# A new order of the lead and of the side steps of a four-row hybrid block

## The reference

```python
x = x + attn_a(layernorm(x))   # per token: q, k, v by heads, elu, k*v summed over heads, q*(kv), two RMS norms, an MLP
x = x + ffn(layernorm(x))      # router, softmax, top 8 of 32 experts, sum of w_e * down(silu(gate) * up)
x = x + attn_b(layernorm(x))   # causal attention, 16 heads of 8, window of 64
x = x + ffn(layernorm(x))
```

## Time and profile before

| what | us |
|---|---|
| median of 3 runs | 997.12 (996.98 to 1001.0) |
| the profiled execution | 996.92 |
| its span, first to last instruction | 995.20 |

### The profile page before, as it was taken

How to read it: one execution, slowest core, us unless ns; L and a number is a source line. 1 busy time by engine, 2 the same in 40 slices (tenths; PEclk the granted TensorE clock), 3 DMA queues, 4 the chain that set the end, 5 groups by cost and what they waited for, 6 DMA issues and landing times.

```text
span 995.2 us, 16822 instructions
## 1 busy us (share of the span) xinstructions
PE 898.2 (90%) x5456; PEld 619.3 (62%) x5456; DVE 663.5 (67%) x1471; ACT 610.0 (61%) x1875; POOL 672.2 (68%) x617
## 2 busy tenths in 40 slices
PE   3276889899999999999999999999999998999998
PEld 1043556677666666587666666677666666767665
DVE  5988777688858747788638846778735347547532
ACT  4344566895665665796674566798465478386432
POOL 7566959576778848766759857856755646645654
PEclk8557999999999999999999999999999999999999
DMA  5004333113442433610433534430334561350352
GB/s 188 0 1 109 73 88 87 43 45 92 104 126 54 123 101 94 158 45 27 95 87 87 129 85 99 128 84 18 73 100 88 127 156 28 78 138 12 85 130 64
DMA packets 64903, 85.75 MB, mean 86 GB/s; under 512 B 5232, under 2 KB 30768, under 8 KB 64560
## 3 DMA queue, kind: packets, MB, share of 16 engines
q1 hardware_dynamic: 64816, 84.68, 35.1%
HBM read 79.39 MB, written 5.28 MB: 85 GB/s over the span
## 4 chain that ended last, share of the span: by engine, by line
PE 55%; ACT 12%; POOL 9%; DVE 6%; issue 5%; DMA 0%; DVEq 0%; SPq 0%; ACTq 0%; POOLq 0%
PE bank L1563 15%; PE bank L1540 8%; PE bank L1542 8%; PE bank L1541 8%; ACT probs L1102 6%; PE bank L1584 3%; POOL work L893 3%; PE bank L1599 3%; PE bank L1613 2%; POOL rstd L837 1%; PE bank L1577 1%; PE bank L1427 1%; DVE work L1325 1%; DVE probsT L1367 1%; POOL kv_terms L850 1%
## 5 line engine op out<-in xcount | busy, mean ns | idle before, releaser
L893 POOL TENSOR_TENSOR work<-work,spread_w 128x512 f32<-128x512 f32 x256 | 336.2, 1324 | 163.8 <-DVE work L1325 160.7
L1325 DVE TENSOR_TENSOR work<-work,bank 128x512 f32<-128x512 f32 x256 | 173.7, 682 | 214.3 <-ACT work L1077 129.3
L1563 PE MATMUL bank<-work,down_w 128*128 128x512 f32 x512 | 263.9, 599 | 12.0 <-POOL work L893 10.0
L1077 ACT ACTIVATE work<-bank 128x512 f32<-128x512 f32 x256 | 150.8, 596 | 177.0 <-PE bank L1542 173.5
L1540 PE MATMUL bank<-z_hi,gate_hi 128*128 128x512 f32 x256 | 166.5, 650 | 5.6 <-ACT work L1077 3.6
L1102 ACT ACTIVATE probs<-bank,neg_max 128x96 f32<-128x96 f32 x512 | 166.0, 383 | 5.8 <-DVE neg_max L1353 3.9
L901 POOL TENSOR_TENSOR probs<-probs,prob_inv 128x768 f32<-128x768 f32 x64 | 94.1, 1471 | 67.5 <-DVE prob_inv L1361 67.5
L1102 ACT ACTIVATION_READ_ACCUMULATOR probs<-bank,neg_max 128x1 f32 x512 | 126.4, 250 | 0.0
L1563 PEld LDWEIGHTS bank<-work,down_w 128*128 128x128 f32 x512 | 94.1, 189 | 44.4 <-POOL work L893 18.1
L1542 PE MATMUL bank<-z_hi,gate_lo 128*128 128x512 f32 x256 | 102.2, 399 | 0.0
L1540 PE MATMUL bank<-z_hi,up_hi 128*128 128x512 f32 x256 | 102.0, 399 | 0.0
(11 more groups left out here) (155 smaller groups left out, 1477.3 us busy)
## 6 DMA issues: line engine op xcount, KB each, us to landing
spread_w<-comb_dram SPq DMA_DIRECT2D x96, 512.0 KB, 6.6
spread_w<-comb_dram SPq DMA_DIRECT2D x128, 128.0 KB, 3.0
vals<-v_dram SPq DMA_DIRECT2D x16, 384.0 KB, 4.1
...
```

The lines of the kernel that those rows point to most:

```text
L893: pool.tensor_tensor(work[:, n % WORK], work[:, n % WORK], spread_w[:, n // EACH % 2, s % EACH], ALU.mult).then_inc(hid_gated, 1)
L1077: act.activation(work[:, n % WORK], bank[GATE_BANKS[ring_of(row, f, s)]], ACT.Silu).then_inc(silu_ready, 1)
L1325: dve.tensor_tensor(work[:, n % WORK], work[:, n % WORK], bank[UP_BANKS[ring_of(row, f, s)]], ALU.mult).then_inc(gated_ready, 1)
L1563: pe.matmul(bank[Y_BANK], down_w[:, c], work[:, n % WORK], start=(c == 0), stop=(c == CH - 1)).then_inc(down_done, 1)
```

## The change

Only the two tables `PLAN` and `AHEAD` are written anew. Both hold the same 655 steps, and no function changes. `AHEAD` has 123 steps instead of 120: `qscale` 0, `attend` 1 and `kvsum` 0 of the next row come in from the first stage. The parts that the prediction speaks of:

```diff
     (0, "first"): {
-        0: own(("h_pow2", 1)) + ahead(("kvsum", 0)) + own(("h_newton2", 1)),
-        1: own(("h_scale", 1)) + ahead(("qscale", 0)) + own(("h_gain", 1)),
-        2: ahead(("wterm", 0)),
-        3: own(("h_sum", 1), ("x_add", 1)) + ahead(("attend", 1), ("wred", 0), ("kvsum", 1)),
-        6: own(("attnT", 1), ("mlp1", 1)),
-        7: own(("mlp2", 1), ("m_stats", 1), ("m_rstd", 1)) + ahead(("wterm", 1)),
-        8: ahead(("wred", 1), ("attend", 2)) + own(("m_apply", 1)) + ahead(("x_stats", 1), ("x_rstd", 1)),
-        10: own(("moe_turn", 1), ("z_hi", 1), ("z_lo", 1)) + ahead(("attend", 3), ("kvsum", 2), ("wterm", 2)),
-        11: ahead(("wred", 2)) + own(("route", 1), ("r_sum", 1), ("top", 1)),
-        12: ahead(("x_apply", 1)) + own(("weigh", 1)) + ahead(("kvsum", 3), ("x_turn", 1)) + own(("comb", 1)),
-        13: ahead(("qkv", 4), ("wterm", 3)),
-        14: own(("cnorm", 1), ("weighT", 1)),
-        15: ahead(("qkv", 5), ("wred", 3)),
+        2: own(("h_pow2", 1), ("h_newton2", 1), ("h_scale", 1)),
+        4: own(("h_gain", 1), ("h_sum", 1)) + ahead(("wterm", 0), ("wred", 0), ("kvsum", 1)) + own(("x_add", 1)),
+        6: own(("attnT", 1), ("mlp1", 1)),
+        7: own(("mlp2", 1), ("m_stats", 1), ("m_rstd", 1)),
+        8: ahead(("wterm", 1)),
+        9: ahead(("x_stats", 1), ("x_rstd", 1)) + own(("m_apply", 1)),
+        10: own(("moe_turn", 1)) + ahead(("attend", 2), ("attend", 3)) + own(("z_hi", 1), ("z_lo", 1)),
+        11: ahead(("wred", 1)) + own(("route", 1), ("r_sum", 1), ("top", 1)) + ahead(("x_apply", 1)) +
+            own(("weigh", 1)) + ahead(("kvsum", 2)),
+        12: ahead(("x_turn", 1)) + own(("comb", 1)),
+        13: ahead(("qkv", 4), ("wterm", 2)) + own(("cnorm", 1)),
+        14: ahead(("wred", 2)) + own(("weighT", 1)) + ahead(("kvsum", 3), ("wterm", 3)),
+        15: ahead(("qkv", 5)),
     },
     (0, "third"): {
-        0: ahead(("h_sq1", 0), ("h_g2", 0), ("h_red1", 0), ("h_newton1", 0), ("h_sq2", 0), ("qkv", 6),
-            ("h_red2", 0), ("h_pow2", 0)),
-        1: ahead(("h_newton2", 0), ("qkv", 7)),
-        3: ahead(("expo", 1)) + own(("y_back", 0), ("s_stats", 0)) + ahead(("h_scale", 0)) + own(("s_rstd", 0)) +
-            ahead(("elu", 1)),
...
+        0: ahead(("wred", 3), ("h_sq1", 0), ("h_red1", 0), ("h_g2", 0), ("h_newton1", 0), ("qkv", 6), ("h_sq2", 0)),
+        1: ahead(("h_red2", 0), ("qkv", 7), ("h_pow2", 0), ("h_newton2", 0)),
+        3: own(("y_back", 0), ("s_stats", 0)) + ahead(("h_scale", 0), ("h_gain", 0), ("h_sum", 0)) +
+            own(("s_rstd", 0)),
+        4: ahead(("expo", 1), ("elu", 1)),
...
     },
     (0, "attn"): {
-        0: ahead(("moe_turn", 0), ("z_hi", 0)),
-        2: ahead(("z_lo", 0)),
...
-        20: own(("proj", 0)) + ahead(("cnorm", 0)),
-        22: ahead(("weighT", 0)),
+        0: ahead(("wred", 4), ("wterm", 5), ("z_hi", 0)),
+        1: ahead(("z_lo", 0)),
+        2: own(("y_back", 1), ("s_stats", 1), ("s_rstd", 1)),
+        4: ahead(("wred", 5)) + own(("s_apply", 1)),
...
+        22: own(("proj", 0)),
+        23: own(("m_stats", 2), ("m_rstd", 2)),
+        25: ahead(("weighT", 0)),
     },
     (1, "third"): {
...
-        6: ahead(("x_turn", 1), ("h_red2", 0), ("h_pow2", 0)),
-        7: back(("moe_turn", 3), ("z_hi", 3)) + ahead(("h_newton2", 0)),
-        8: back(("z_lo", 3)) + ahead(("h_scale", 0)),
-        9: back(("route", 3), ("r_sum", 3)) + ahead(("h_gain", 0)),
...
+        6: back(("moe_turn", 3), ("z_hi", 3), ("z_lo", 3)),
...
+        9: back(("route", 3), ("r_sum", 3)) + ahead(("h_gain", 0)) + back(("top", 3), ("weigh", 3)),
...
     },
     (1, "fourth"): {
...
-        7: ahead(("z_lo", 0), ("wterm", 5), ("attend", 6)),
-        8: ahead(("route", 0), ("r_sum", 0)) + own(("s_apply", 1)),
-        9: own(("seq_turn", 1)) + ahead(("top", 0), ("wred", 5)) + own(("bias", 1)),
...
-        12: ahead(("cnorm", 0), ("wred", 6)),
-        13: ahead(("weighT", 0), ("kvsum", 7)),
...
+        7: ahead(("route", 0), ("attend", 6), ("attend", 7), ("r_sum", 0), ("top", 0), ("kvsum", 5), ("wterm", 5),
+            ("wred", 5)),
...
+        10: ahead(("comb", 0), ("wterm", 6), ("wred", 6)) + own(("keys", 1)) + ahead(("cnorm", 0)),
...
     },
     (1, "attn"): {
-        8: back(("y_back", 3)),
-        26: own(("proj", 0)),
+        0: ahead(("weighT", 0)),
+        5: back(("y_back", 3)),
+        9: ahead(("wred", 7)) + own(("bias", 1)) + ahead(("h_sq1", 1)),
+        13: ahead(("h_g2", 1)),
+        15: ahead(("h_red1", 1), ("h_sq2", 1)),
+        26: ahead(("h_newton1", 1)),
     },
     (2, "attn"): {
-        8: back(("y_back", 3)),
-        26: own(("proj", 0)),
+        0: ahead(("weighT", 0), ("kvsum", 7)) + own(("bias", 1)),
+        2: ahead(("wterm", 7)) + back(("y_back", 3)),
+        6: ahead(("wred", 7)),
+        10: ahead(("h_sq1", 1)),
+        11: ahead(("h_g2", 1)),
+        14: ahead(("h_red1", 1)),
+        23: ahead(("h_newton1", 1)),
     },
     (3, "first"): {
-        0: back(("m_stats", 2), ("m_rstd", 2)) + own(("h_sq1", 1), ("h_g2", 1)),
-        1: own(("h_red1", 1)),
-        2: own(("h_newton1", 1), ("h_sq2", 1)),
-        3: back(("proj", 1)) + own(("h_red2", 1), ("h_pow2", 1)),
...
+        1: back(("proj", 0)),
+        2: own(("h_sq2", 1)) + back(("m_stats", 2), ("m_rstd", 2)) + own(("h_red2", 1)),
...
     },
     (3, "attn_lo"): {
-        5: own(("y_back", 1)),
-        6: own(("s_stats", 1), ("s_rstd", 1)),
+        0: back(("y_back", 2)),
+        3: own(("y_back", 1)),
+        6: own(("s_stats", 1)),
+        7: own(("s_rstd", 1)),
+        10: own(("s_apply", 1)) + back(("weighT", 3)),
+        14: own(("seq_turn", 1)),
     },
     (3, "attn_hi"): {
-        5: back(("y_back", 3)),
+        2: back(("y_back", 3)),
+        5: own(("weighT", 2)),
     },
...
 AHEAD = (
-    own(("masks", 0), ("x_stats", 0), ("x_rstd", 0), ("x_apply", 0), ("x_stats", 1), ("lam", 0), ("x_turn", 0),
-        ("qkv_first", 0), ("qkv_first", 1), ("masks", 1), ("qkv_first", 2), ("elu_first", 0), ("w_hi", 0),
-        ("elu_first", 1), ("qkv_first", 3), ("x_rstd", 1), ("elu_first", 2), ("attend", 0), ("attend", 1),
-        ("kvsum", 0), ("wterm", 0), ("wred", 0), ("attend", 2), ("x_apply", 1), ("kvsum", 1), ("wterm", 1),
-        ("x_turn", 1), ("elu_first", 3), ("attend", 3), ("kvsum", 2), ("qkv", 4), ("wred", 1), ("wterm", 2),
-        ("kvsum", 3), ("qkv", 5), ("wred", 2), ("wterm", 3), ("wred", 3), ("h_sq1", 0), ("h_g2", 0), ("w_lo", 0),
-        ("qkv", 6), ("qkv", 7), ("h_red1", 0), ("h_newton1", 0), ("h_sq2", 0), ("expo", 1), ("h_red2", 0),
-        ("h_pow2", 0), ("w_hi", 1), ("h_newton2", 0), ("elu", 1), ("h_scale", 0), ("h_gain", 0)) +
-        ahead(("x_stats", 0)) + own(("attend", 4), ("h_sum", 0)) + ahead(("x_rstd", 0)) + own(("qscale", 1),
-        ("kvsum", 4), ("attnT", 0), ("x_add", 0), ("wterm", 4), ("attend", 5), ("mlp1", 0)) +
-        ahead(("x_apply", 0)) + own(("wred", 4), ("w_lo", 1), ("mlp2", 0)) + ahead(("x_turn", 0)) +
-        own(("m_stats", 0), ("kvsum", 5), ("m_rstd", 0), ("wterm", 5), ("m_apply", 0), ("wred", 5)) +
-        ahead(("qkv_next", 0), ("qkv_next", 1)) + own(("attend", 6), ("attend", 7), ("moe_turn", 0), ("kvsum", 6),
-        ("z_hi", 0), ("z_lo", 0), ("route", 0), ("early", 0), ("wterm", 6), ("r_sum", 0), ("top", 0), ("weigh", 0),
-        ("comb", 0), ("wred", 6), ("cnorm", 0), ("kvsum", 7)) + ahead(("qkv_next", 2)) + own(("wterm", 7),
-        ("weighT", 0), ("wred", 7)) + ahead(("qkv_next", 3)) + own(("h_sq1", 1), ("h_g2", 1), ("h_red1", 1),
-        ("early", 1), ("masks", 2), ("h_newton1", 1), ("h_sq2", 1)) + ahead(("expo", 0), ("elu", 0)) +
-        own(("early", 2), ("early", 3), ("lead", 0), ("early", 4), ("lead", 1), ("lead", 2), ("lead", 3),
-        ("lead", 4), ("early", 5), ("h_red2", 1), ("lead", 5)) + ahead(("attend", 0))
+    own(("masks", 0), ("x_stats", 0), ("x_rstd", 0), ("x_apply", 0), ("x_turn", 0), ("lam", 0),
+        ("qkv_first", 0), ("qkv_first", 1), ("qkv_first", 2), ("elu_first", 0), ("masks", 1), ("attend", 0),
+        ("x_stats", 1), ("elu_first", 1), ("qkv_first", 3), ("w_hi", 0), ("kvsum", 0), ("elu_first", 2),
+        ("elu_first", 3), ("wterm", 0), ("attend", 1), ("x_rstd", 1), ("wred", 0), ("kvsum", 1), ("wterm", 1),
+        ("attend", 2), ("kvsum", 2), ("attend", 3), ("wred", 1), ("x_apply", 1), ("wterm", 2), ("x_turn", 1),
+        ("w_lo", 0), ("qkv", 4), ("kvsum", 3), ("wred", 2), ("wterm", 3)) + ahead(("x_stats", 0)) + own(("qkv", 5),
+        ("wred", 3), ("w_hi", 1), ("h_sq1", 0), ("h_red1", 0), ("h_g2", 0), ("h_sq2", 0)) + ahead(("x_rstd", 0)) +
+        own(("h_newton1", 0), ("h_red2", 0), ("h_pow2", 0), ("h_newton2", 0), ("h_scale", 0), ("qkv", 6),
+        ("qkv", 7), ("expo", 1), ("h_gain", 0), ("elu", 1), ("h_sum", 0), ("attend", 4), ("qscale", 1),
+        ("attnT", 0), ("x_add", 0), ("kvsum", 4), ("wterm", 4), ("mlp1", 0), ("mlp2", 0), ("m_stats", 0),
```

(46 more changed lines are left out.)

309 lines of the change are left out of this document (129 added, 180 removed).

## The result

The changed kernel takes 970.89 us (median of four runs, 967.24 to 972.73) beside 997.05 of the kernel before (996.76 to 1001.0): a ratio of 0.9724, interval 0.9687 to 0.9762, so 26 us faster. The forecast was 990.6 with a range of 976 to 1004: the direction was right, the size was not, and the result lies outside the range. The profiled execution took 970.32, its span 968.5, against 995.2 before.

The account below looks back on a forecast made before the run. TensorE, 90% busy, was taken to set the pace in MLP stages and ScalarE's exponentials in attention. Terms -3.5 - 4.5 + 1 + 6.5 - 6 = -6.5 on 996.9 gave 990.4, 990.6 on the median's scale; range 976 to 1004.

Parts of the forecast that it names:

- The lead: Stretch before the main loop: the gated of chunk 6 comes at about 101.4 instead of 104.93, -3.5 us.
- the walk: In the lead, the new list followed engine by engine with old durations: h_sum near 48.5, combT about 81, first hidden about 87.
- The held Newton steps: In the lead, five of six VectorE operations slowed beside POOL's subtractions would run in the clear, about 4.8 us.
- the masks' new place: In the lead, masks move behind attend 7 into POOL's idle time, so the late weighT is just covered, 3 us left.
- Row 0's first and third stage: Waits for zT, comb and the qkv copy go, 3.7 us, plus half the low-clock time: -4.5, ends -8.2 and 0.
- half of the low stretch: In row 0's first and third stage, half of the 3.41 us at the lower clock goes.
- Later attention: Attention of rows 1 to 3 grows by added ScalarE steps summing to 6.7 us: +6.5, ends +2 and +8.3.
- the price of one for one: In later attention, each added ScalarE microsecond lengthens the stage at least as much; from row 0 against row 1, 8.1 for 6.8.
- the rival: In attention, VectorE's moved steps are paid one for one on top, 13.3 instead of +1: 1002.9 us, slower, chance 0.20.
- Later MLP stages: Two thirds of the 9.2 us of TensorE waits for hidden, z_lo and comb go: -6, ends -9.2 and +3.
- The lumps that I feared: In the MLP stages, crowded slots keep waits as before, 0 instead of -6: 996.6 us, chance 0.25.
- Row 0's attention: VectorE steps of 4.7 us come in, covered by idle time but able to hold a score maximum: +1, ends 0 and 4.7.

Follow-up runs that it names:

- e17_masks: Changed kernel with x_stats in slot 5 and, in the lead, masks 2 put back behind h_g2 1; first hidden at 86.3, first down at 87.7 us.
- e5_wlo: Changed kernel with x_stats in slot 5 and, in the lead, w_lo 0 put back behind h_g2 0; first down at 87.4 us.
- e1_lead: Kernel before with only the new lead list (AHEAD), later tables old; 989.51 us, ratio 0.9898.
- The pads: Kernel before with extra unused ScalarE or VectorE steps in attention of rows 1 and 2; ScalarE's 12 made each stage 1.2 us longer, VectorE's four 4.3 in row 1.
- e14_pad_start: Kernel before with extra 1.22 us VectorE reductions in attention: row 1 two (hooks 0, 2), 0.3 us longer; row 2 four (0, 2, 6, 14), 5.3 longer.
- e10_early: Kernel before with z_lo one slot sooner in two third stages and weighT one slot later in two fourth stages; 997.26 us, ratio 0.9991.
- e2_row0: Kernel before with the new lead list and the new tables of period 0, periods 1 to 4 old; 983.32 us, ratio 0.9858.
- e13_masks: Changed kernel with x_stats in slot 5 and, in the lead, masks 2 put behind early 1, which left POOL's queue the same; first down at 84.4 us.

## Why the prediction was wrong

By the stages the forecast missed 20 us: 3.5 in the lead, 5.9 in row 0's two stages, 5.6 in later attention, 4.8 in the later MLP stages with row 1's first among them. Only in later attention was the mechanism wrong; elsewhere terms were sized wrongly or left out.

**The lead (-3.5; measured -7.0).** The parts were the right ones, but the walk put the weights too late. It put h_sum at 48.5 since w_hi 1 and x_stats "now come ahead" of it, 1.2 us each. They had stood ahead of it before too, as the old timeline shows:

```profile
43.64 1.22 DVE L1191 CAST up_hi<-spread_w 128x2048 fp32r<-128x2048 f32 x1
...
47.96 0.86 DVE L1160 BATCH_NORM_STATS2 stats<-x_buf 128x6 f32<-128x128 f32 x4
```

I charged as new what was there, 2.4 us; and h_sum was not held, 0.9. It began 0.14 us ahead of POOL's attend (44.81 and 44.95). By the Trainium skill, "SBUF — State Buffer", section "Who interferes with whom", the one that is issued first has the port; which one that would be I had left open. The trace agrees: h_sum took 0.69 us and attend 2.75, where the next attend took 2.33. The held Newton steps I had put at 4.8 us; the rows give 4.4 over the five.

The step that failed is the next one: the walk let z_lo come out within a microsecond of the old and combT, behind it, at 81. z_lo came 3.6 us sooner, as the kernel before and the changed one show, and combT at 75.95, 5 us sooner than forecast:

```profile
66.18 0.69 DVE L1279 TENSOR_TENSOR z_lo<-bank,z_hi 128x512 fp32r<-128x512 f32 x1
```

```profile
62.62 0.68 DVE L1258 TENSOR_TENSOR z_lo<-bank,z_hi 128x512 fp32r<-128x512 f32 x1
```

From combT to the first hidden I had some 6 us, and 5.7 to 6.1 is what it takes where the transfer ends last. So the transfer was ready just as POOL came from its attends, at 81.9 instead of 87. Both had to be early for that: with the masks back POOL is late (first hidden 86.3, e17_masks), with w_lo back combT is late (85.8, e5_wlo). I had named the masks' new place, and then hidden its gain behind a transfer that I had too late.

**Row 0's first and third stage (-4.5; measured -10.4).** I counted the waits for zT, comb and the qkv copy, 3.7 us, and half of the low stretch. The term that failed is the wait for hidden, 4.5 us and the largest row: I put its gain at nothing without a reason. It went (4.5 to 0.4), and most of it by the lead: with the new lead and the old tables (e1_lead) 1.4 us are left of it. That for zT stayed (1.0). By the rows, TensorE's waits from the first down to row 0's attention fell from 11.1 to 3.7: 7.4 of the 10.4. Another 1.8 is the low stretch, which is gone in other executions with the old tables too and is no gain of the change; I had counted half of it. The change itself made the two stages 8.6 us shorter.

**Later attention (+6.5; measured +0.9: 0.8, 0.6, -0.9, 0.4).** This is the step whose mechanism failed: the price of one for one for ScalarE's steps, 6.7 us by the sum, where the stages grew by 0.9. The price of one for one came from row 0's attention against row 1's: 8.1 us longer with 6.8 us more ScalarE work. But the same two rows differ by 5.2 us on VectorE and 6.0 on TensorE, and I gave the whole to ScalarE. What row 0's 8.1 us are made of was not tried. The pads show the reverse: ScalarE steps cost a fifth of their length, VectorE steps in mid-stage 0.6 to 0.9 of it. In the middle of a stage the price that I gave the rival (VectorE's steps paid one for one) was nearly right; what the rival missed is that the change puts kvsum and wterm at hooks 0 and 2, where there is room (e14_pad_start, row 1). For hooks 6 and 14 the pads leave it open, since that stage fell into low clock. Row 3's s_apply and seq_turn cost nothing since hooks 10 and 14 of a stage of four tiles come after its last exponentials (s_apply began at 813.9, they ended at 813.98).

**Later MLP stages (-6; measured -10.8, or -17.5 without row 1's first).** The kind of cause was right, its size was not. The waits for hidden, z_lo and comb fell from 9.2 to 1.5, more than the two thirds that I took. And I had drawn the bound from three kinds of wait. TensorE's rows from row 1's second stage to the end sum to 25.8 before and 13.3 after: 12.5 us went, some 5 of them in other kinds (for probs 2.7, probsT, yT, elu). With a fifth on top for what the rows leave out (e10_early) that is an estimate of 15.0 of the 16.6 by which this stretch, attention included, became shorter; 1.6 us stay unexplained. The lumps that I feared show nowhere: row 1's fourth stage has no wait for hidden behind slot 7 and is 2.6 us shorter. The largest new wait was of a kind that I had not looked for, a load behind a step moved on another engine, by way of SP's queue.

**Row 0's attention (+1; measured +0.7).** The number is near by luck: the 46.5 us hold 3.4 at the low clock. At full clock the new order took 45.4 (e2_row0, e13_masks) and the old 45.8, so the stage became 0.4 shorter and not 1 longer.
